# Attention loop of a graph kernel: the front scan turned inside the window sums, next queries ahead of the averaged values, destination indices loaded a group sooner

## The chip, the core and the metric

The kernel runs on one core of a Trainium2 chip. The metric is the device time of one execution in microseconds (us); lower is better. Engines are named as in the profile: PE is TensorE (PEld its weight loads), DVE VectorE, ACT ScalarE, POOL GpSimd, SP SyncE, which issues most DMAs.

## What is computed

3125 nodes of 128 features and 53125 edges sorted by destination (25000 edges both ways and the self loops). Layer 0 is graph attention with 8 heads of 16; layer 1 a degree-normalised sum with a hyperbolic map. Cut to layer 0, which is where the change lies:

```python
h = jnp.maximum(_layernorm(x), 0.0)
Q, K, V = (h @ Wq + bq), (h @ Wk + bk), (h @ Wv + bv)          # (3125, 8, 16) each
scores = jnp.sum(Q[dst] * K[src], axis=-1) * scale + (edge_attr @ We + be)
exp_s = jnp.exp(scores - segment_max(scores, dst)[dst])
probs = exp_s / (segment_sum(exp_s, dst) + 1e-10)[dst]
x = x + segment_sum(probs[:, :, None] * V[src], dst) @ Wo + bo
```

Layer 1 follows with the same edges: `x + expmap0(segment_sum(h1[src] * dinv[src] * dinv[dst], dst))`.

## The kernel before

The edges are cut into 32 groups (`GROUPS`) of 13 tiles (`T`) of 128 edges. One lap of the attention loop handles one group g, and the engines work on it side by side, joined by semaphores alone; each engine's order is written out by hand in its own `step`.

**POOL** (`gather`) fetches K and V of each edge's source: 13 indirect DMAs of 128 rows of 1 KB per group, in chunks of 4, 4, 4 and 1 tiles (`CH`), into `kv[:, b]` with b = g % 2. Below, gather 0 to gather 12 are those of one group. Ahead of gather 7 it waits until gathers 4 to 6 have landed (line 667). Ahead of gathers 0 and 8 it waits for `s_wv`, that is until `weigh(g - 2)` has read that half of the buffer.

**PE** turns the window's 128 query rows into one row per edge (`query`, `ps_q <- ST, qwin`), in four chunks, adds the edge bias (`bias`), and sums the weighted values of group g-1 by destination (`window_sums`, 13 tiles of two passes each, then the two small carry products that set `s_rc`). It counts source degrees (`ps_f <- oh_lo, oh_hi`) and turns small tiles for the scans.

**DVE** in `step(g)`: `scores` multiplies and reduces chunk by chunk (`prod`, `sc`), adds the bias and scans the running maximum of each head over the 13 tiles (`f1`); `scan_partitions` scans over the 128 partitions, `backward`, `scan_partitions_back` and `shifted` do the same from the other end, so that `z` is the score less its segment's maximum. `combine` carries the sums R of group g-1 and averages them (`agn`); it also held the one-hot matrices of a coming group: `shift_matrix`, `edge_one_hots` and `row_one_hots` (`ST <- dloc_b, imj`). ACT takes the exponent, and `weigh` multiplies V by it in two pieces (`wv <- kv, wv`). `new_rows(g - 1)` adds the residual once PE has made the product with Wo (`s_o`).

**SP** loads for the coming groups, in a loop whose every step also stores the rows of group g-2 and so waits for `new_rows`: edge features, `dloc_b` (destination indices spread over 128 partitions), query rows, then the store, then the residual rows.

Of the kernel before, what the change touches and what calls it, by code (L numbers as in the profile page):

```python
# [27 lines left out]
P = 128  # L28
# [23 lines left out]
TB = CH[2][0]  # L52

# [73 lines left out]
def build(nc, x, src_t, dst_t, dst_before, dst_after, dst_first, dst_run, src_run, attr, wqkv, bqkv, we, be, wo, bo, w1t, b1,  # L127
# [12 lines left out]
    with ExitStack() as ctx:  # L140
# [331 lines left out]
        def _(sp):  # L472
# [49 lines left out]
            def load_edges(g, b):  # L522

                if not (known(g) and g < 2):
                    wait_apart(sp, s_bias, g - 1, (s_base, 1))
                sp.dma_start(attr_s[:, b, 0:3, :],
                             attr[bass.ds(g, 1), 0:3 * P, :].rearrange("o (k p) e -> p (o k) e", p=P)).then_inc(s_attr[b], 16)
                sp.dma_start(attr_s[0:EF, b, 3, :],
                             attr[bass.ds(g, 1), 3 * P:T * EF, :].rearrange("o p e -> p (o e)")).then_inc(s_attr[b], 16)
                load_dloc(g, b)  # L530
                w = base_of(g)
                if not (known(g) and g < 2):
                    wait_apart(sp, s_qt, NCH * (g - 1), (s_base, 1))
                sp.dma_start(qwin[:, b, :], q_tab[bass.ds(w, P), :]).then_inc(s_qwin[b], 16)
# [17 lines left out]
            with sp.If_eq(in_order, 1):  # L552
                load_edges(0, 0)
                load_edges(1, 1)
                load_nodes(0, 0)
# [4 lines left out]
                with sp.Fori(1, GROUPS // 2) as n:  # L560
                    for b in range(2):
                        load_edges(2 * n + b, b)
                        store_nodes(2 * n + b - 2, b)
                        load_nodes(2 * n + b, b)
# [160 lines left out]
        def _(dve):  # L725
# [200 lines left out]
            def scores(g, b, st, more):  # L926
# [88 lines left out]
            def combine(g, b, st, edges, more, next_st):  # L1015

# [4 lines left out]
                if more:  # L1021
                    shift_matrix(g + 2, b, s_rc, s_S)
# [4 lines left out]
                if more:  # L1027
                    edge_one_hots(g + 2, b, s_S, TA)
                    row_one_hots(g + 2, b)
                st.sync()  # L1030
                V.tensor_tensor(R[:, b, :], R[:, b, :], ps_r[:, 0:C + 1], ALU.add).then_inc(s_R, 1)
                if edges:
                    scan_partitions(g + 1, 1 - b, next_st)
                dve.wait_ge(s_R, g + 1)
                r3 = R[:, b, 0:C].rearrange("p (h e) -> p h e", h=H)
                st.mark(V.tensor_scalar(rden[:].unsqueeze(2), r3[:, :, DH:DH + 1], 1e-10, None, ALU.add))
                if edges:
                    first_row(g + 1, next_st)
                st.sync()
# [19 lines left out]
            def step(g, b, edges=True, nodes=True, more=True, far=True):  # L1059
# [3 lines left out]
                if edges:  # L1063
                    scores(g, b, A, more)
                if nodes:
                    combine(g - 1, 1 - b, B, edges, edges and more, A)
                    B.check(NB)
                else:
                    scan_partitions(g, b, A)
                    first_row(g, A)  # L1070
                    shift_matrix(g + 1, 1 - b, s_rc, s_S)
                    edge_one_hots(g + 1, 1 - b, s_S, TA)
                    row_one_hots(g + 1, 1 - b)
# [6 lines left out]
                if nodes:  # L1080
                    new_rows(g - 1, 1 - b)
# [275 lines left out]
        def _(act):  # L1357
# [42 lines left out]
            def step(g, b, nodes=True, more=True):  # L1400
                if more:
                    one_hots(g + 1, 1 - b, (0, 1))
                if nodes:
# [3 lines left out]
                carry_factor(g)  # L1407
                weights(g)
# [90 lines left out]
        def _(pe):  # L1499
# [58 lines left out]
            def window_sums(g, b, bias_read=True):  # L1558
# [11 lines left out]
                if bias_read:  # L1570
# [5 lines left out]
            def step(g, b, edges=True, nodes=True, more=True):  # L1576
                if edges:
                    query(g, b, (2, 3))
                if nodes:
                    window_sums(g - 1, 1 - b, edges)  # L1580
                if edges:

# [7 lines left out]
                    pe.wait_ge(s_v1, g + 1)  # L1590
                    M.transpose(p_v1, f1[:, :, T - 1], ident[:]).then_inc(s_v1T, 1)
                if edges:
                    wait_apart(pe, s_cf, g + 1, (s_part, 1))
                    M.transpose(p_c1, c1[:, b, 0:P], ident[0:H, 0:H]).then_inc(s_cfT, 1)
                if nodes:
                    pe.wait_ge(s_agn, g)
                    M.transpose(ps_f[:, 0:D], agn[:], ident[:]).then_inc(s_agTp, 1)
                if edges:
# [3 lines left out]
                    M.transpose(p_c2, c2[:, 1:P + 1], ident[0:H, 0:H]).then_inc(s_cbT, 1)  # L1602
                if nodes:
# [5 lines left out]
                if edges and more:  # L1609
                    query(g + 1, 1 - b, (0,))  # L1610
                    bias(g + 1, 1 - b, (0, 1))
                    query(g + 1, 1 - b, (1,))
# [171 lines left out]
```

## Time and profile before

| | us |
|---|---|
| median of three runs (lowest, highest) | 1085.56 (1083.99, 1094.68) |
| the profiled execution | 1088.42 |
| its span in the trace | 1086.2 |
| first gather of the attention loop starts | 48.90 |
| last gather of the attention loop starts | 709.46 |
| busy in the span: PE, PEld, DVE, ACT, POOL | 883.0, 734.1, 734.9, 394.2, 656.0 |

The attention loop takes from 48.90 to about 735 of the span; what follows is layer 1, which the change doesn't touch. In the rows of a timeline the columns are start, duration, engine, line, operation, output and inputs, and in brackets how long the engine had been idle and for what. The busy shares are averages over both layers, so the loop is read from its own stretches.

### The profile page before, as it was taken

What the parts mean: (1) busy time and instruction counts of PE and PEld (TensorE: products, weight loads), DVE (VectorE), ACT (ScalarE), POOL (GpSimd) and SP (SyncE); (2) the same over time, 40 slices, a digit from 0 to 9 for tenths busy, and PEclk for the clock granted to TensorE, in tenths of its full rate; (3) what the DMA queues carried; (4) which work ended last, traced back from release to release, by engine and by line L of the source; (5) the groups of instructions that cost most, each with busy time, mean ns of one, the idle gap of its engine ahead of it and who ended that gap; (6) DMA issues with size and microseconds to landing.
All of it is one profiled execution on the core that took longest, in us unless ns stands there. A gap on an engine that the chain in (4) does not pass through costs nothing.

```text
span 1086.2 us, 20358 instructions
## 1 busy us (share of the span) xinstructions
PE 883.0 (81%) x4860; PEld 734.1 (68%) x4860; DVE 734.9 (68%) x2772; ACT 394.2 (36%) x1091; POOL 656.0 (60%) x629
## 2 busy tenths in 40 slices
PE   4548878888897988887987898873479999999996
PEld 2237867876886886886876787772267575757574
DVE  8746576576666666666657657748857676768675
ACT  1532233233223224224223323302725565556551
POOL 0167767766776676776776776610267666667663
PEclk9866676676666666667667667676789999999999
DMA  5553443443443443443444353401212222222221
GB/s 151 168 169 91 137 118 108 144 118 110 134 126 108 130 132 108 126 135 113 119 137 117 107 146 114 115 26 65 79 49 60 64 59 61 60 60 60 63 61 47
DMA packets 87845, 111.18 MB, mean 102 GB/s; under 512 B 20787, under 2 KB 65791, under 8 KB 87807
## 3 DMA queue, kind: packets, MB, share of 16 engines
q0 software_dynamic: 26624, 68.20, 21.8%
q1 hardware_dynamic: 61191, 42.64, 13.9%
q8 instruction: 12, 0.20, 0.1%
q14 instruction: 18, 0.15, 0.0%
HBM read 99.83 MB, written 10.95 MB: 102 GB/s over the span
## 4 chain that ended last, share of the span: by engine, by line
POOL 25%; PE 23%; issue 19%; DVE 16%; DMA 14%; ACT 1%; DVEq 1%; POOLq 0%; ACTq 0%; SPq 0%
POOL kv L668 18%; DMA kv<-kv_tab,idx 10%; POOL kv L703 7%; PE ps_r L1697 5%; PE ps_f L1705 3%; PE ps_q L1554 2%; PE ps_r L1566 2%; DMA kv<-hs_tab,idx 2%; PE ps_s L1680 2%; PE ps_q L1680 2%; DVE ST L880 2%; DVE wv L1012 1%; DVE sc L941 1%; PE ps_f L1608 1%; PE ps_f L1607 1%
## 5 line engine op out<-in xcount | busy, mean ns | idle before, releaser
L668 POOL DMA_INDIRECT kv<-kv_tab,idx x416 | 458.3, 1102 | 251.2 <-issue 167.8
L703 POOL DMA_INDIRECT kv<-hs_tab,idx x208 | 197.3, 949 | 166.2 <-DMA hs_tab<-qkv 69.5
L1378 ACT ACTIVATE S<-iota,nloc 128x128 f32<-128x128 f32 x384 | 122.1, 389 | 383.0 <-PE ps_r L1566 381.9
L1554 PE MATMUL ps_q<-qwin,ST 128*128 128x128 f32 x832 | 205.5, 430 | 2.0 <-DVE ST L880 2.0
L935 DVE TENSOR_TENSOR prod<-kv,ps_q 128x512 f32<-128x512 f32 (+1 forms) x128 | 74.6, 583 | 172.8 <-DMA kv<-kv_tab,idx 103.9
L1554 PEld LDWEIGHTS ps_q<-qwin,ST 128*128 128x128 f32 x832 | 186.1, 329 | 3.0 <-issue 2.1
L1566 PE MATMUL ps_r<-wv,S 128*128 128x137 f32 x832 | 140.8, 342 | 1.8 <-DVE wv L1012 1.8
L1566 PEld LDWEIGHTS ps_r<-wv,S 128*128 128x128 f32 x832 | 140.7, 254 | 2.1 <-DVE wv L1012 2.1
L1697 PE MATMUL ps_r<-qkv,xt 128*128 128x128 f32 x800 | 101.7, 292 | 21.2 <-ACT xt L1468 21.2
L1697 PEld LDWEIGHTS ps_r<-qkv,xt 128*128 128x128 f32 x800 | 98.7, 206 | 27.4 <-ACT xt L1468 25.6
L1538 PEld LDWEIGHTS ps_c<-we,attr_s 128*128 128x128 f32 (+1 forms) x256 | 62.9, 321 | 19.9 <-DMA attr_s<-in_attr 12.1
L1538 PE MATMUL ps_c<-we,attr_s 128*128 128x32 f32 (+1 forms) x256 | 65.8, 378 | 11.8 <-DMA attr_s<-in_attr 11.8
L941 DVE TENSOR_REDUCE sc<-prod 128x32 f32<-128x512 f32 (+1 forms) x128 | 71.5, 580 | 0.0
L1457 ACT ACTIVATE S<-iota,nloc 128x128 f32<-128x128 f32 x208 | 67.1, 392 | 0.0
L1012 DVE TENSOR_TENSOR wv<-kv,wv 128x1024 f32<-128x1024 f32 x64 | 62.1, 1007 | 0.2 <-ACT wv L1397 0.2
L1381 ACT ACTIVATE S<-S 128x512 f32<-128x512 f32 x96 | 60.5, 630 | 3.0
L1587 PE MATMUL ps_f<-oh_lo,oh_hi 128*50 128x64 bf16 x416 | 56.8, 303 | 0.0
L1705 PE MATMUL ps_f<-kv,S 128*128 128x128 f32 x416 | 51.0, 281 | 3.8 <-DMA kv<-hs_tab,idx 3.7
L1283 DVE TENSOR_SCALAR ST<-bwd_reset 128x800 bf16<-128x800 f16 x112 | 50.3, 449 | 4.5 <-PE ps_c L1680 4.5
L1284 DVE TENSOR_SCALAR wv<-iota_b,bwd_reset 128x128 bf16<-128x128 bf16 x208 | 52.5, 252 | 0.0
L1705 PEld LDWEIGHTS ps_f<-kv,S 128*128 128x128 f32 x416 | 49.3, 197 | 4.5 <-issue 3.6
L1587 PEld LDWEIGHTS ps_f<-oh_lo,oh_hi 128*50 128x50 bf16 x416 | 49.0, 172 | 0.8
(245 smaller groups left out, 1282.7 us busy)
## 6 DMA issues: line engine op xcount, KB each, us to landing
dloc_b<-dloc_tab SPq DMA_DIRECT2D x32, 416.0 KB, 5.1
kv<-kv_tab,idx POOLq DMA_INDIRECT x416, 4.0
attr_s<-in_attr SPq DMA_DIRECT2D x32, 192.0 KB, 2.9
kv<-hs_tab,idx POOLq DMA_INDIRECT x208
kv_tab<-qkv SPq DMA_DIRECT2D x5, 640.0 KB, 4.0
x_tab<-x SPq DMA_DIRECT2D x32, 64.5 KB
qwin<-q_tab SPq DMA_DIRECT2D x32, 64.0 KB, 4.1
xwin<-in_x SPq DMA_DIRECT2D x32, 64.0 KB, 2.0
```

The source lines that it names most:

```text
L668: pool.indirect_dma_start(out=kv[:, b, t, :], out_offset=None, in_=kv_tab, in_offset=bass.IndirectOffsetOnAxis(ap=idx[:, b, t:t + 1], axis ...
L703: pool.indirect_dma_start(out=kv[:, j, t, 0:D], out_offset=None, in_=hs_tab, in_offset=bass.IndirectOffsetOnAxis(ap=idx[:, j, t:t + 1], ax ...
L935: V.tensor_tensor(prod[:, c % 2, 0:w, :], kv[:, b, t0:t1, 0:D], ps_q[c % 2][:, 0:w * D].rearrange("p (t d) -> p t d", d=D), ALU.mult).then ...
L941: st.mark(V.tensor_reduce(sc[:, :, t0:t1].rearrange("p h t -> p t h"), prod[:, c % 2, 0:t1 - t0, :].rearrange("p t (h d) -> p t h d", d=DH ...
L1012: V.tensor_tensor(w4[:, t0:t1, :, 0:DH], kv[:, b, t0:t1, D:2 * D].rearrange("p t (h d) -> p t h d", d=DH), w4[:, t0:t1, :, DH:DH + 1].to_b ...
L1378: A.activation(S[:, b, t, :], iota[:], ACT.Abs, bias=nloc[:, g, t:t + 1] if known(g) else nloc[:, bass.ds(g, 1), t:t + 1].rearrange("p g t ...
L1538: mm = M.matmul(p_bias[:, 4 * H * k:4 * H * k + w], attr_s[0:r, b, k, :], we4[0:r, 0:w], start=False, stop=k == 3)
L1554: mm = M.matmul(ps_q[c % 2][:, (t - t0) * D:(t - t0 + 1) * D], ST[:, b, t, :], qwin[:, b, :], start=True, stop=True)
L1566: mm = M.matmul(ps_r[:, 0:C + 1], S[:, b, t, :], wv[:, t, :], start=(t == 0), stop=(t == T - 1))
L1587: mm = M.matmul(ps_f[0:HI, 3 * D:3 * D + LO], oh_hi[:, b, :, t], oh_lo[:, b, :, t], start=(t == 0), stop=(t == T - 1))
L1697: M.matmul(ps_r[:, 0:D], counts[:, i, :], hs_t[:, i, :], start=(i == 0), stop=False)
L1705: M.matmul(sum_banks[1][:, 0:D], S[:, j, t, :], kv[:, j, t, 0:D], start=(t == 0), stop=False)
```

## The change

In the PE's `window_sums(g - 1)` the transpose of group g's front scan (`f1`) is put ahead of the last two of the 13 tiles; before it stood behind the degree counts. The counts now stand behind the transpose of the partition scan. `query(g + 1, chunk 0)` is put ahead of the transpose of `agn`, and the product with Wo behind `query(g + 1, chunk 1)`. DVE takes the partition scan before the carry, the averaging behind `z`, `weigh` right behind the averaging, and the one-hots of the edges, `first_row`, `shift_matrix` and `new_rows` behind `weigh`. `row_one_hots` moves to the start of a step, behind the first product, and makes them for group g+1 there (before: for group g+1 in `combine` of the same step). ACT takes `carry_factor` and `weights` ahead of `agg_copy` and the last third of the one-hots. SP issues the load of `dloc_b` for group g+1 where it issued that for group g. No instruction is added or taken out of a lap.

```diff
+TV = T - 2
@@ SP
-                load_dloc(g, b)
...
+                def turn(g, b, more=True):
+                    if more:
+                        load_dloc(g + 1, 1 - b)
+                    load_edges(g, b)
+                    store_nodes(g - 2, b)
+                    load_nodes(g, b)
@@ DVE scores
                 product(0)
+                if more:
+                    row_one_hots(g + 1, 1 - b)
@@ DVE step
                 if edges:
                     scores(g, b, A, more)
+                if edges:
+                    scan_partitions(g, b, A)
                 if nodes:
-                    combine(g - 1, 1 - b, B, edges, edges and more, A)
...
+                    carry(g - 1, 1 - b, B)
                 if edges:
                     backward(g, b, A)
+                if nodes:
+                    add_sums(g - 1, 1 - b, B)
...
                     shifted(g, b, A)
                 if nodes:
+                    average(g - 1, 1 - b, B)
+                    B.check(NB)
+                if edges:
+                    weigh(g, b)
+                    first_row(g, A)
+                    if more:
+                        shift_matrix(g + 1, 1 - b, s_rc, s_S)
+                        edge_one_hots(g + 1, 1 - b, s_S, TA)
+                if nodes:
                     new_rows(g - 1, 1 - b)
                 if edges:
                     add_counts(g)
                     factor(g)
-                    weigh(g, b)
@@ ACT step
+                carry_factor(g)
+                weights(g)
                 if nodes:
                     agg_copy(g - 1)
                 if more:
                     one_hots(g + 1, 1 - b, (2,))
-                carry_factor(g)
-                weights(g)
@@ PE window_sums
                 for t in range(T):
                     if t == TB:
                         pe.wait_ge(s_wv, 2 * g + 2)
+                    if edges and t == TV:
+                        turned_front(g + 1)
```

DVE, one step of the loop, from the scan to the next product, before (`fb` and `R` are the carry, `rden` and `agn` the average, `x` the new rows):

```order
L957 SCALAR_TENSOR_TENSOR f<-fwd_reset,sc 128x104
L905 TENSOR_TENSOR oh_lo<-lo_f,rep_hi 128x832
...
L880 TENSOR_SCALAR ST<-dloc_b,imj 128x1664
L1031 TENSOR_TENSOR R<-R,ps_r 128x137
L967 COPY c<-c 8x1
...
L999 TENSOR_TENSOR z<-sc,tmp 128x104
L1050 TENSOR_TENSOR x<-ps_f,xwin 128x128
L1051 COPY x<-R 128x1
L912 TENSOR_TENSOR od_s<-od_s,ps_f 50x64
L1004 SCALAR_TENSOR_TENSOR facd<-ident,fac 8x8
L1012 TENSOR_TENSOR wv<-kv,wv 128x8x8x16
```

and the same stretch now, up to the next step's products:

```order
L1012 TENSOR_TENSOR z<-sc,tmp 128x104
L1047 TENSOR_SCALAR rden<-R 128x8
L1048 RECIPROCAL rden<-rden 128x8
L1049 TENSOR_TENSOR agn<-R,rden 128x128
L1025 TENSOR_TENSOR wv<-kv,wv 128x8x8x16
L1025 TENSOR_TENSOR wv<-kv,wv 128x5x8x16
L996 TENSOR_SCALAR isf<-iota,ofirst 8x128
L879 TENSOR_SCALAR shift<-imj,delta 128x128
L883 TENSOR_TENSOR S<-dloc,iota 128x128
L1058 TENSOR_TENSOR x<-ps_f,xwin 128x128
```

`ST` (now line 891) has left the middle of the step for the place between the next step's first two products; `wv` no longer stands behind `x`.

PE, from the end of one step into the next, before:

```order
L1607 MATMUL ps_f<-bo_s,ones_row 128x128
L1608 MATMUL ps_f<-wo_s,agT 128x128
L1554 MATMUL ps_q<-qwin,ST 128x128 x4
```

and now:

```order
L1568 MATMUL ps_q<-qwin,ST 128x128 x4
L1623 MATMUL ps_f<-ident,agn 128x128
L1548 MATMUL ps_c<-be_r,ones_row 128x104
L1549 REGISTER_ALU
L1552 MATMUL ps_c<-we,attr_s 128x32 x2
L1568 MATMUL ps_q<-qwin,ST 128x128 x4
L1630 REGISTER_ALU
L1631 MATMUL ps_f<-bo_s,ones_row 128x128
L1632 MATMUL ps_f<-wo_s,agT 128x128
```

The product with Wo, on which `new_rows` waits, now stands behind two query chunks and half of the bias.

## Rows read from the trace of the kernel before

**Rows 1.** Page, part 4: shares of the chain that ended last, by engine.
```profile
POOL 25%; PE 23%; issue 19%; DVE 16%; DMA 14%; ACT 1%; DVEq 1%; POOLq 0%; ACTq 0%; SPq 0%
```

**Rows 2.** Windows: exactly 24 laps; busy us and (instructions) of each engine, clock, DMA.
```profile
173.12:670.15 497.03, 426.23 (x2114) 380.92 (x2113) 328.76 (x984) 150.12 (x432) 345.31 (x312) 0.66 0.42 123
```

**Rows 3.** Waits in 150 to 700 us: waiter, releaser, us in total, times, longest.
```profile
DVE prod L935 <- DMA kv<-kv_tab,idx: 88.1, 27, 3.8
POOL kv L668 <- DMA kv<-kv_tab,idx: 66.1, 26, 2.9
DVE prod L935 <- PE ps_q L1554: 54.8, 27, 2.2
```

**Rows 4.** Timeline, POOL and DVE, one lap from gather 11 on (origin 418.99).
```profile
418.99 0.95 POOL L668 DMA_INDIRECT kv<-kv_tab,idx  x1 [0.30 <-issue]
...
423.83 0.69 DVE L935 TENSOR_TENSOR prod<-kv,ps_q 128x512 f32<-128x512 f32 x1 [3.35 <-DMA kv<-kv_tab,idx]
...
428.06 1.53 POOL L668 DMA_INDIRECT kv<-kv_tab,idx  x1 [0.30 <-issue]
...
428.40 1.08 DVE L880 TENSOR_SCALAR ST<-dloc_b,imj 128x1664 f32<-128x1664 bf16 x1
...
429.90 0.94 POOL L668 DMA_INDIRECT kv<-kv_tab,idx  x1 [0.30 <-issue]
...
433.40 0.94 POOL L668 DMA_INDIRECT kv<-kv_tab,idx  x1 [2.56 <-DMA kv<-kv_tab,idx]
...
434.69 0.29 DVE L1050 TENSOR_TENSOR x<-ps_f,xwin 128x128 f32<-128x128 f32 x1 [0.52 <-PE ps_f L1608]
...
435.23 1.94 DVE L1012 TENSOR_TENSOR wv<-kv,wv 128x1024 f32<-128x1024 f32 x2
...
435.90 2.09 POOL L668 DMA_INDIRECT kv<-kv_tab,idx  x1 [0.30 <-issue]
```

**Rows 5.** Timeline, POOL and then DVE, gathers 8 and 9 of an earlier lap.
```profile
227.74 0.95 POOL L668 DMA_INDIRECT kv<-kv_tab,idx  x1 [0.30 <-issue]
229.76 1.37 POOL L668 DMA_INDIRECT kv<-kv_tab,idx  x1 [1.08 <-issue]
...
228.35 1.94 DVE L1012 TENSOR_TENSOR wv<-kv,wv 128x1024 f32<-128x1024 f32 x2
```

**Rows 6.** Timeline, SP's DMA issues around gather 11 (a store, `dloc_b`, the query rows).
```profile
414.85 0.35 SPq L549 DMA_DIRECT2D x_tab<-x  x1
...
418.17 0.34 SPq L519 DMA_DIRECT2D dloc_b<-dloc_tab  x1
...
419.47 0.34 SPq L534 DMA_DIRECT2D qwin<-q_tab  x1
```

**Rows 7.** Timeline, PE: window sums, counts, product with Wo, query 0, bias, query 1.
```profile
422.16 4.49 PE L1566 MATMUL ps_r<-wv,S 128*128 128x137 f32 x26
...
427.38 1.78 PE L1587 MATMUL ps_f<-oh_lo,oh_hi 128*50 128x64 bf16 x13
...
433.06 0.78 PE L1607 MATMUL ps_f<-bo_s,ones_row 1*128 1x128 f32 x2
...
434.15 1.83 PEld L1554 LDWEIGHTS ps_q<-qwin,ST 128*128 128x128 f32 x8
...
436.20 0.50 PEld L1534 LDWEIGHTS ps_c<-be_r,ones_row 1*128 1x128 f32 x2 [0.22 <-issue]
...
437.69 1.83 PEld L1554 LDWEIGHTS ps_q<-qwin,ST 128*128 128x128 f32 x8
```

**Rows 8.** Timeline, the end of the loop: last gather, last scan, its transpose, last `weigh`.
```profile
709.46 0.95 POOL L668 DMA_INDIRECT kv<-kv_tab,idx  x1 [0.30 <-issue]
...
714.28 0.37 DVE L957 TENSOR_TENSOR_SCAN f<-fwd_reset,sc 128x104 f32<-128x104 f32 x1
...
718.61 0.28 PE L1591 MATMUL ps_b<-ident,f 128*8 128x128 f32 x1
...
724.13 1.94 DVE L1012 TENSOR_TENSOR wv<-kv,wv 128x1024 f32<-128x1024 f32 x2
```

More of the change, by code:

```diff
@@ L552, in _ @@
             with sp.If_eq(in_order, 1):
+                load_dloc(0, 0)
+                load_dloc(1, 1)
                 load_edges(0, 0)
                 load_edges(1, 1)
+                load_dloc(2, 0)
                 load_nodes(0, 0)
@@ L559, in _ @@
                 sp.dma_start(x2_tab[N:NPAD, :], zero_rows[:]).then_inc(s_pad, 16)
[L560 to L564, printed above, removed]
+                def turn(g, b, more=True):
[4 more added lines that the diff above has]
+                    load_nodes(g, b)
+                with sp.Fori(1, GROUPS // 2 - 1) as n:
+                    turn(2 * n, 0)
+                    turn(2 * n + 1, 1)
+                turn(GROUPS - 2, 0)
+                turn(GROUPS - 1, 1, more=False)
                 store_nodes(GROUPS - 2, 0)
@@ L1013, in weigh, with carry @@
                                     w4[:, t0:t1, :, DH:DH + 1].to_broadcast([P, t1 - t0, H, DH]), ALU.mult).then_inc(s_wv, 1)
-            def combine(g, b, st, edges, more, next_st):
+            def carry(g, b, st):
                 dve.wait_ge(s_rc, g + 1)
@@ L1556, in query, with turned_front, window_sums @@
                     mm.then_inc(s_qt, 1)
-            def window_sums(g, b, bias_read=True):
+            def turned_front(g):
+                pe.wait_ge(s_v1, g + 1)
+                M.transpose(p_v1, f1[:, :, T - 1], ident[:]).then_inc(s_v1T, 1)
+            def window_sums(g, b, edges=True):
                 pe.wait_ge(s_wv, 2 * g + 1)
@@ L1569, in window_sums @@
                     pe.wait_ge(s_R, g)
-                if bias_read:
+                if edges:
                     pe.wait_ge(s_sc, g + 2)
@@ L1580, in step @@
                     window_sums(g - 1, 1 - b, edges)
+                elif edges:
+                    turned_front(g)
                 if edges:
+                    wait_apart(pe, s_cf, g + 1, (s_part, 1))
+                    M.transpose(p_c1, c1[:, b, 0:P], ident[0:H, 0:H]).then_inc(s_cfT, 1)
                     pe.wait_ge(s_oh, 2 * g + 2)
@@ L1589, in step @@
                     mm.then_inc(s_hist, 1)
[L1590 to L1598, printed above, removed]
                     pe.wait_ge(s_v2, g + 1)
@@ L1602, in step @@
                     M.transpose(p_c2, c2[:, 1:P + 1], ident[0:H, 0:H]).then_inc(s_cbT, 1)
+                if edges and more:
+                    query(g + 1, 1 - b, (0,))
+                if nodes:
+                    pe.wait_ge(s_agn, g)
+                    M.transpose(ps_f[:, 0:D], agn[:], ident[:]).then_inc(s_agTp, 1)
+                if edges and more:
+                    bias(g + 1, 1 - b, (0, 1))
+                    query(g + 1, 1 - b, (1,))
                 if nodes:
@@ L1609, in step @@
                 if edges and more:
-                    query(g + 1, 1 - b, (0,))
-                    bias(g + 1, 1 - b, (0, 1))
-                    query(g + 1, 1 - b, (1,))
                     bias(g + 1, 1 - b, (2, 3))
```

22 lines of the change are left out of this document (4 added, 18 removed).

## The prediction, made before the changed kernel was run

> **What bounds the kernel now.** I read the chain of waits first. It gives POOL 25%, PE 23%, issue 19%, DVE 16% [rows 1], and in the loop it runs through DVE's `weigh` back to POOL, which looks like a ring through all engines that a better order could shorten. The other views speak against that. The windows give 24 laps in 497.03 us, 20.71 us a lap, with DVE at 66% and PE, whose busy time is modelled, at 86% [rows 2]. In the waits DVE stands still for landing gathers 88.1 us and for PE's queries 54.8 us, over 5 us a lap, while POOL waits only for its own DMAs, 66.1 us in 26 laps [rows 3]. The timeline shows why. A gather takes 0.95 us and the next starts 0.30 us later, 1.25 in all; gather 7 starts 3.50 us after gather 6, since it waits until that one has landed (429.90 to 433.40) [rows 4]. So a lap of POOL costs 13 x 1.25 = 16.25, plus 3.50 - 1.25 = 2.25, together 18.5 us, whatever the others do. The missing 2.2 us are stretched gathers: in the lap shown 1.53 instead of 0.95 beside `ST`, and 2.09 beside `weigh` [rows 4].
>
> What stretches them is DVE. `weigh` runs from 435.23 to 437.17; the gather that started at 435.90 ends at 437.99, 0.82 behind it [rows 4]. `ST` runs from 428.40 to 429.48; the gather of 428.06 ends at 429.59, 0.11 behind it [rows 4]. A gather already 0.61 us old when `weigh` starts (227.74 against 228.35) is not touched, and the next one is then held: it starts at 229.76 and ends at 231.13, 0.84 behind `weigh` [rows 5]. So POOL sets the lap, and DVE matters only by where these two operations fall upon gathers. I read no wait of POOL on a semaphore of DVE: the buffer that gather 0 of g+2 needs is free when `weigh(g)` has done its first piece (at 16.2 + 1.2 in a lap whose gather 11 is the origin), and that gather starts at 2.5 + 20.6 = 23.1, almost 6 us later.
>
> **Where the moved parts come to lie.** Times from here on are us behind the start of gather 11, and F is when DVE takes the product of chunk 2, for which gather 11 must have landed. Before, F = 423.83 - 418.99 = 4.84 and `weigh` starts at 16.24, which is F + 11.4 [rows 4].
>
> *The scan to `weigh`.* The front scan ends at F + 3.4 as before. PE has reached the eleventh tile by then (see the ring below), so the transpose follows at once (0.28, duration as in [rows 8]); then the last two tiles, 2/13 of 4.49 = 0.7 [rows 7], and the two carry products, about 0.8 by their rows: `s_rc` at F + 5.2. DVE does its partition scan inside that time, the carry by F + 5.7, the correction and the second scan by F + 6.7. The degree counts, 1.8 us [rows 7], now stand on PE from F + 5.3 to 7.1 and hold the second transpose back by 0.4. From that transpose to the end of `z` it took 2.3 us before; that gives F + 9.3, and three averaging operations give F + 10.0 for `weigh`, 1.4 sooner. ACT's exponent is covered by the averaging; ACT's first two thirds of the one-hots, 3.9 us from F + 4.5, end before z is there.
>
> *The queries.* Query 0, bias and query 1 started at 434.15, 436.20 and 437.69 [rows 7], so they take 2.05, 1.49 and about 1.75. They now run from F + 8.2, with the transpose of `agn` (0.35) between: F + 13.9. The Wo product takes 1.5 from its start (433.06) to the read by `x` (434.69) [rows 4, 7], so `new_rows`, which was done before `weigh`, waits until F + 15.4. DVE then is idle for almost 3 us; behind it are queued the counts, the factor and the next step's products.
>
> *The ring.* Product 0 comes at F + 16.1, `ST` from F + 16.8 to F + 17.9, product 1 to F + 18.6, the reduction to F + 19.2, and there the next chunk 2 can be taken. A ring of 19.2 us is below 20.7, so its slack hides the late `new_rows`; of the 5 us of waits in [rows 3] about 1.5 are left. If this cover were gone, each us would count 32 times.
>
> *The DMAs.* SP's burst (store, residual rows, then loads) started at -4.14 and ended with the query rows at 0.48, `dloc_b` at -0.82, just ahead of gather 11's landing [rows 4, 6]. It now follows `new_rows` and starts at F + 16.1 - 20.7 = F - 4.6, some 3 us later. Gather 6, with no burst beside it, lands about 2.7 us after its start, gather 11 needs 4.84 [rows 4]; so F should fall into 3.0 to 4.8. I take 3.6, nearer to the clean one. `dloc_b` itself, issued a lap sooner, has a whole lap to land; nothing waits for it.
>
> *What POOL pays.* For `weigh` at F + 10.0 = 13.6: gather 7 would start at 13.5 to 13.8. If it starts inside `weigh` or less than about 0.3 before it, it ends 0.83 behind it: with F = 3.0 the stall covers part (1.15 lost), with F = 3.7 nothing (2.0 lost). If `weigh` comes later than that, gather 7 is spared and gather 8 pays 1.0 to 1.8. Before, the mean of the gathers beside `weigh` was 1.56 over 25 laps by my count of their starts. I take 1.5. For `ST`, 1.08 long, ending a gather 0.11 behind it: a gather that is s old at its start loses s + 0.24, so 0.24 to 1.1, or nothing if it fell into the stall; it now starts near F + 16.8 = 20.4, close to gather 11, far from the stall. I take 0.6, the 0.59 of the lap shown [rows 4]. Shift and edge one-hots, now right behind `weigh`, and the source one-hots: 0.25, between 0 and 0.5. Sum 2.35 against 2.2 before: a lap of 20.85, +0.14, and over 32 laps +4.5 us.
>
> A rule speaks to this. The Trainium skill (SBUF — State Buffer, section on who interferes with whom) says that a two-input tensor operation takes only the read side shared with GpSimd, that 2-port modes take both, and that the loser is blocked until the other's end, about 0.115 us for the descriptors to finish. For `ST` the trace agrees (0.11); for `weigh` the gather ends 0.82 behind, so it seems to be held at its start. By the page's 0.115 each `weigh` would cost 0.7 less, before and after alike, and the sum would not change.
>
> *The end of the loop.* In the last lap no gathers hold DVE. The last scan starts at 714.28, but its transpose stands behind the sums and the counts and comes at 718.61, 4.0 us after the scan's end; `weigh` follows at 724.13 [rows 8]. With the transpose inside the sums it comes about 0.5 after the scan; the carry, still 1.3 behind, and the rest as above put `weigh` at 721.6. That is 2.5 us, for once on the path, between 1.5 and 3.5.
>
> **The sum** is +4.5 - 2.5 = +2 us. Against the profiled execution (1088.42, span 1086.2) that is 1090.4; against the median of the runs, 1085.56, it is 1087.6, and I predict 1088: no change.
>
> **Rivals.**
> *Faster: the blocks fall well.* If the burst moves out of gather 11's way, F = 3.0, `weigh` costs 1.15, and `ST` finds a gather young (0.24), small ones 0.1: 1.5 instead of 2.2, a lap of 20.0, 32 x -0.71 - 2.5 = -25, 1060 us. For it: F has 1.8 us of room. Against: F must fall by nearly all of it and `ST` be lucky too. Chance 0.22. The ring (19.2) forbids anything below about 1035.
> *Slower: `ST` in the open.* This is the rule of the same page turned on the change: an operation that takes the shared ports should lie where POOL is not working, and the change does the opposite. Before, `ST` at 9.41 lay one gather ahead of the stall; now each `ST` may cost 1.1, with `weigh` upon the start of gather 7 (1.9) and the two one-hots behind it (0.2): 3.2, a lap of 21.7, +32 - 2.5, 1115 us; with half of the laps so, 1101. It decides once the blocks pass 2.65 a lap. Chance 0.18.
> *The change does nothing to the laps*: all of it stays in DVE's slack and only the end gains, 1083. Chance 0.10.
> The forecast keeps 0.50.
>
> **Numbers.** About 1% (11 us) is what a measurement of this kernel can tell from no change. One lap's uncertainty of 0.4 us is 13 us, so the forecast gives 0.07 to faster and 0.05 to slower. Faster 0.07 + 0.20 = 0.27; slower 0.05 + 0.17 = 0.22; same 0.51. The range 1064 to 1108 takes in most of both rivals. The forecast's own range is 1076 to 1100.
>
> **What would show it.** Right: POOL's only wait is still that ahead of gather 7, 3.5 us after gather 6; `weigh` starts 1.4 us sooner behind product 2; `x` waits about 3 us for the Wo product while DVE's wait for landing gathers shrinks; the lap stays at 20.5 to 21.1; `ST` falls beside gathers 10 to 12 and stretches them. Wrong: a wait of gathers 0 or 8 on `weigh`; a ring above 20.7, seen as DVE taking chunk 2 without waiting for its landing; a stall ahead of gather 7 that differs from 3.5 us, because the later burst meets gathers 4 to 6.

## The result: faster, by what `weigh` costs POOL

The changed kernel takes 1062.28 us (median of 4 runs, 1059.48 to 1064.59), the kernel before 1087.67 on the same chip: ratio 0.9753, with a 95% interval of 0.971 to 0.9795. Two further comparisons (`a1_changed` and `a2_changed` below, each beside the kernel before) gave 0.9788 (0.9733 to 0.9844) and 0.9766 (0.9738 to 0.9794). The forecast, 1088 and no change, was wrong; 1062 lies below its range too. It came out close to the rival "the blocks fall well" (1060, chance 0.22), but not for that rival's reason.

The profiled execution has a span of 1061.0 us. Its chain of waits, by engine, against [rows 1]:

```profile
POOL 43%; issue 22%; DMA 14%; PE 11%; DVE 8%; POOLq 1%; ACT 0%; DVEq 0%; SPq 0%; ACTq 0%
```

The chain now runs mostly on POOL and its DMAs; PE and DVE, before 23% and 16%, are down to 11% and 8%. The windows over 24 whole laps (us, then busy us and instructions of PE, PEld, DVE, ACT and POOL, clock, DMA share, GB/s), which answer to [rows 2]:

```profile
171.41:647.38 475.97, 418.74 (x2120) 372.88 (x2119) 337.27 (x986) 150.30 (x432) 325.78 (x312) 0.66 0.46 128
```

A lap takes 475.97 / 24 = 19.83 us instead of 20.71. PE and DVE do the same work (a mean of 17.45 and 14.05 us a lap, before 17.76 and 13.70) at the same granted clock, 0.66. POOL's busy time for the same 312 gathers fell from 345.3 to 325.8 us, 0.81 a lap: nearly all of the 0.88 of the lap. So the gathers themselves became shorter. The waits from 150 to 680 us, against [rows 3]:

```profile
POOL kv L679 <- issue: 99.6, 321, 1.1
DVE x L1058 <- PE ps_f L1632: 85.6, 26, 3.5
POOL kv L679 <- DMA kv<-kv_tab,idx: 68.2, 27, 2.7
...
DVE prod L946 <- DMA kv<-kv_tab,idx: 19.8, 14, 2.7
```

POOL still waits for its own DMAs alone (68.2 us in 27 laps, before 66.1 in 26). DVE's waits have moved from landing gathers (88.1 to 19.8 us) to the Wo product, 3.3 us a lap.

Where a gather became shorter shows in two laps of the timeline, POOL's rows and then DVE's (start, duration, line, names, idle time before it):

```profile
403.09 1.08 POOL L679 DMA_INDIRECT kv<-kv_tab,idx  x1 [0.30 <-issue]
...
409.54 1.50 POOL L679 DMA_INDIRECT kv<-kv_tab,idx  x1 [0.30 <-issue]
...
440.73 1.57 POOL L679 DMA_INDIRECT kv<-kv_tab,idx  x1 [2.51 <-DMA kv<-kv_tab,idx]
...
401.92 0.29 DVE L1049 TENSOR_TENSOR agn<-R,rden 128x128 f32<-128x128 f32 x1
402.13 1.95 DVE L1025 TENSOR_TENSOR wv<-kv,wv 128x1024 f32<-128x1024 f32 x2
...
408.01 0.29 DVE L1058 TENSOR_TENSOR x<-ps_f,xwin 128x128 f32<-128x128 f32 x1 [3.35 <-PE ps_f L1632]
...
409.14 1.07 DVE L891 TENSOR_SCALAR ST<-dloc_b,imj 128x1664 f32<-128x1664 bf16 x1
...
440.26 1.95 DVE L1025 TENSOR_TENSOR wv<-kv,wv 128x1024 f32<-128x1024 f32 x2
```

`weigh` is two operations, one for 8 tiles and one for 5, and the row joins them. The tile's view keeps them apart (shortest, median and longest in ns, first and last start); before, and now:

```profile
L1012 DVE TENSOR_TENSOR wv<-kv,wv x2: 806/1006/1207, 435.2 to 436.4; 128x1024 f32<-128x1024 f32 x1, 128x640 f32<-128x640 f32 x1
```

```profile
L1025 DVE TENSOR_TENSOR wv<-kv,wv x2: 817/1018/1218, 440.3 to 441.4; 128x1024 f32<-128x1024 f32 x1, 128x640 f32<-128x640 f32 x1
```

Now the first piece ends at 440.26 + 1.22 = 441.48 and the gather beside it at 442.30, 0.82 behind the FIRST piece and 0.09 behind the second; the same in the other lap (403.35, 404.17). Before, the gather ended 0.82 behind the SECOND piece, 1.56 behind the first [rows 4]. By the records this holds throughout: before, in 30 of 31 laps with a gather beside `weigh`, it ended 0.83 behind the second piece; now, in 27 of 31, 0.82 behind the first, and in the other 4 it had started only when the second piece had started too, and ended 0.82 behind that. I say that a gather is **held** through both pieces, or is **let in** between them.

What each DVE operation costs POOL, in us a lap (what the gathers beside it last beyond the 0.945 us of an undisturbed one, laps 6 to 30, from the records):

| kernel | `weigh` | `ST` | others | lap |
|---|---|---|---|---|
| before | 1.43 | 0.51 | 0.15 | 20.69 |
| changed | 0.38 | 0.57 | 0.29 | 19.79 |
| changed, `a1_changed` and `a2_changed` | 0.43, 0.52 | 0.59, 0.54 | 0.26, 0.26 | 19.84, 19.87 |

With the prediction's 18.5 us for an undisturbed lap of POOL these rows add up to the laps within 0.1.

### The profile page after: what moved, and what is told of

It is laid out like the page before. It is cut to its first block, busy times and chain, and to the rows that moved or that the text cites. A ratio compares the mean times of both kernels' runs of the same rounds, so it can differ in the third digit from the quotient of the medians.

```text
span 1061.0 us, 20346 instructions
## 1 busy us (share of the span) xinstructions
PE 873.9 (82%) x4860; PEld 724.1 (68%) x4860; DVE 745.2 (70%) x2772; ACT 394.6 (37%) x1091; POOL 631.2 (59%) x629
## 4 chain that ended last, share of the span: by engine, by line
POOL 43%; issue 22%; DMA 14%; PE 11%; DVE 8%; POOLq 1%; ACT 0%; DVEq 0%; SPq 0%; ACTq 0%
POOL kv L679 29%; POOL kv L714 14%; DMA kv<-kv_tab,idx 9%; DMA kv<-hs_tab,idx 4%; PE ps_q L1568 2%; PE ps_r L1587 2%; PE ps_f L1612 1%; DVE st L759 1%; DMA kv_tab<-qkv 1%; PE ps_f L1726 1%; DVE qkv L787 1%; DVE qkv L1281 1%; PE ps_r L1718 1%; PE ps_q L1530 1%; PE ps_f L1631 0%
## 5 line engine op out<-in xcount | busy, mean ns | idle before, releaser
L679 POOL DMA_INDIRECT kv<-kv_tab,idx x416 | 433.6, 1042 | 250.7 <-issue 166.8
L1568 PE MATMUL ps_q<-qwin,ST 128*128 128x128 f32 x832 | 198.6, 418 | 26.7 <-DVE prod L946 23.6
L1568 PEld LDWEIGHTS ps_q<-qwin,ST 128*128 128x128 f32 x832 | 174.3, 311 | 32.1 <-DVE prod L946 24.9
L1587 PE MATMUL ps_r<-wv,S 128*128 128x137 f32 x832 | 145.7, 343 | 0.0
L1587 PEld LDWEIGHTS ps_r<-wv,S 128*128 128x128 f32 x832 | 143.1, 254 | 0.3
L946 DVE TENSOR_TENSOR prod<-kv,ps_q 128x512 f32<-128x512 f32 (+1 forms) x128 | 74.3, 581 | 43.0 <-DMA kv<-kv_tab,idx 29.6
L1058 DVE TENSOR_TENSOR x<-ps_f,xwin 128x128 f32<-128x128 f32 x32 | 9.4, 292 | 101.5 <-PE ps_f L1632 101.5
```

What stands on the lines that cost most here:

```text
L679: pool.indirect_dma_start(out=kv[:, b, t, :], out_offset=None, in_=kv_tab, in_offset=bass.IndirectOffsetOnAxis(ap=idx[:, b, t:t + 1], axis ...
L946: V.tensor_tensor(prod[:, c % 2, 0:w, :], kv[:, b, t0:t1, 0:D], ps_q[c % 2][:, 0:w * D].rearrange("p (t d) -> p t d", d=D), ALU.mult).then ...
L1568: mm = M.matmul(ps_q[c % 2][:, (t - t0) * D:(t - t0 + 1) * D], ST[:, b, t, :], qwin[:, b, :], start=True, stop=True)
```

## The experiments

Each group of kernels ran on one chip with the kernel before beside it. In the first two groups (e1 to e3; e4b, e5, e6, e7) the kernel before took 1184 and 1210 us instead of 1087; why is not known, and the argument uses from them only ratios and which operation a gather's end follows.

### Is it the place of `weigh`, or what is beside it?

**e1**, the kernel before with `weigh` directly behind `z`:

```
                     shifted(g, b, A)
+                    weigh(g, b)
...
-                    weigh(g, b)
```

> The kernel before, with weigh alone moved: right behind z, ahead of new_rows, the counts and the factor. Theory 'sooner': the lap shrinks by what weigh gains on the landing of gather 11 (about 0.65 us, since it still waits for ACT's exponent), 31 laps, so -20 us. Theory 'port between the pieces': in the kernel before a gather caught by weigh ends 0.82 behind its second piece, in the changed kernel 0.82 behind its first; weigh here starts after an idle gap, as in the one lap of before where the gather did end 0.82 behind the first piece, so I expect that here in all laps, 0.74 a lap, -20 to -28 us. The trace tells them apart: end of the caught gather against the ends of the two pieces.

Ratio 1.0163 (1.009 to 1.0235). The three gathers that `weigh` held up ended 0.82 behind the first piece: let in, in the old order. Yet it was slower: `weigh` fell beside gathers 12 and 0, and gather 0 waited for the semaphore of `weigh`'s first piece, 74.7 us in 27 laps over the kernel. The prediction had given that gate almost 6 us of room.

**e2**, the kernel before with `add_counts` between the two pieces of `weigh`:

> The kernel before, with add_counts (one SBUF input, one PSUM input) moved in between the two pieces of weigh; weigh starts 0.13 us sooner, its second piece ends as before or 0.1 later. 'Port between the pieces': the held gather gets through after the first piece, 0.74 less a lap, -20 to -25 us (about 1064). 'Sooner': 0.1 a lap at most, 1085. 'POOL waits for the semaphore of weigh's first piece': 0.1 a lap too, 1085.

Ratio 1.0032 (0.9989 to 1.0074), and the gathers were held to 0.83 behind the second piece all the same. So a foreign operation between the pieces does not let them in.

**e3**, the kernel before with `factor` and `add_counts` exchanged:

> The kernel before, with factor and add_counts swapped, so that weigh follows the counts instead of the 8x8 factor operation, at the same time. If the operation right ahead of weigh decides whether the port is let go between the pieces: 0.74 less a lap, about 1064. 'Sooner' and 'semaphore': no change, 1086.

Ratio 0.9983 (0.9941 to 1.0025), held as before in 25 laps.

**e4b**, the changed kernel with two short operations directly ahead of `weigh` (PE takes the factor together with the row mask, so both had to move):

```
                 if edges:
+                    first_row(g, A)
+                    factor(g)
                     weigh(g, b)
-                    first_row(g, A)
...
-                    factor(g)
```

> The changed kernel with the row mask (first_row) and factor moved from behind new_rows to directly ahead of weigh; everything else as changed. Before the change a gather caught by weigh ended 0.83 us behind weigh's SECOND piece in 30 of 31 laps, after it 0.82 us behind the FIRST piece in 27 of 31; what stands directly ahead of weigh on DVE differs (before: factor, an 8 x 8 operation; after: the averaging product, 128 x 128). Theory A (what runs directly ahead of weigh decides whether a caught gather gets through between the pieces): factor is ahead again, the caught gathers end 0.83 behind the second piece, the first piece lasts 1.207 instead of 1.219, the lap grows by 0.5 to 0.75 us and the time by 15 to 24 us, to 1077 to 1086. Rival B (it is the place of weigh in the lap, beside gathers 7 to 10 in the open part, that decides): the gathers go on ending 0.82 behind the first piece, and the time stays within 6 us of the changed kernel, 1062.

The hold came back, longer than before. Timeline of one lap:

```profile
300.46 2.50 POOL L679 DMA_INDIRECT kv<-kv_tab,idx  x1 [0.30 <-issue]
...
299.79 1.94 DVE L1025 TENSOR_TENSOR wv<-kv,wv 128x1024 f32<-128x1024 f32 x2
301.66 0.27 DVE L879 TENSOR_SCALAR shift<-imj,delta 128x128 f32<-128x128 f32 x1
301.86 0.27 DVE L883 TENSOR_TENSOR S<-dloc,iota 128x128 f32<-128x128 f32 x1
```

The gather ended at 302.96: 1.23 behind `weigh`, 0.83 behind `S`, the last of the operations queued without a gap behind it. So in 30 laps. Only in the first lap, where `weigh` stood behind a gap, was the gather let in. Ratio 0.9867 (0.9789 to 0.9946).

**e7**, the kernel before with the averaging product repeated into a spare tile directly ahead of `weigh`:

> The kernel before with one operation added: the averaging product done a second time, into a spare tile, directly ahead of weigh and behind factor (0.2 us of DVE a lap, nobody reads it). Theory A (the operation directly ahead of weigh decides whether a caught gather gets through between weigh's pieces): the caught gathers now end 0.82 behind the first piece, the first piece lasts 1.219 instead of 1.207, and the lap falls by 0.5 to 0.75 us: 1065 to 1073, faster than before although an operation was added. Rival B (only the place in the lap or the order of the other steps matters): they still end 0.83 behind the second piece, and the time is that of before within 6 us, 1082 to 1094.

Theory A, as put there, fell: the seven gathers caught behind the first lap were held to the end of the second piece. The kernel was faster (0.9773, 0.9688 to 0.9858); in the profiled execution `weigh` caught a gather in only 8 laps and cost 0.23 us a lap. I draw nothing from that ratio.

### What decides

**e8**, the kernel before with `factor` behind `weigh`:

> The kernel before with factor (an 8 x 8 scalar_tensor_tensor) moved from directly ahead of weigh to directly behind it. So far a caught gather was held through every operation queued behind a factor (before: to the end of weigh's second piece; with factor ahead of weigh in the changed kernel: even to the end of the edge one-hots, 1.22 behind weigh, in 30 of 32 laps), also where another operation stood between factor and weigh (the spare product, the counts); without factor ahead (the changed kernel) it got through at the end of the first piece. Theory A (the factor's operation makes DVE keep the gathers out until a chain of back-to-back operations ends): here weigh has no factor ahead, caught gathers end 0.82 behind the FIRST piece, the lap falls by up to 0.74 us; where weigh lies beside gathers at all, that is 10 to 24 us less than before, ratio 0.98 to 0.99. Rival (something else in the order of the changed kernel lets them through): they still end 0.83 behind the second piece, ratio 0.995 to 1.005.

Held as before in 28 laps, ratio 0.9977 (0.9954 to 0.9999): theory A fell again. It isn't the factor. Ahead of `weigh` now stood `x`, its copy and the counts, without a gap. Behind `weigh` the factor and product 0 followed without a gap either, and yet the gather ended 0.82 behind `weigh` and not behind them.

**e9**, the changed kernel with one short operation more:

```
+                    V.scalar_tensor_tensor(out=spare[:], in0=ident[0:H, 0:H], scalar=imj[0:H, 0:1],
+                                           in1=ident[0:H, 0:H], op0=ALU.mult, op1=ALU.subtract)
                     weigh(g, b)
```

> The changed kernel with one 8 x 8 scalar_tensor_tensor on constants, written to a spare tile and read by nobody, added directly ahead of weigh (0.14 us of DVE a lap). Theory A (that operation makes DVE keep the gathers out): caught gathers end 0.8 us behind the end of the edge one-hots (1.22 behind weigh's second piece) instead of behind the first piece, so each costs up to 1.1 us more: the lap grows by 0.7 to 1.1 us, the time by 20 to 35 us against the changed kernel. Rival (only the place of weigh matters): the ends stay at 0.82 behind the first piece and the time within 6 us of the changed kernel.

1081.0 us where the changed kernel of the same group took 1062.9: an operation of 0.21 us on 8 x 8 numbers that nobody reads costs 18 us. The timeline:

```profile
184.91 2.51 POOL L680 DMA_INDIRECT kv<-kv_tab,idx  x1 [2.46 <-DMA kv<-kv_tab,idx]
...
184.23 0.29 DVE L1050 TENSOR_TENSOR agn<-R,rden 128x128 f32<-128x128 f32 x1
184.44 0.21 DVE L1091 SCALAR_TENSOR_TENSOR spare<-ident,imj 8x8 f32<-8x8 f32 x1
184.57 1.94 DVE L1026 TENSOR_TENSOR wv<-kv,wv 128x1024 f32<-128x1024 f32 x2
```

The gather ends at 187.42, 0.91 behind `weigh` (I had said 1.22), so in 30 laps, and `weigh` costs POOL 1.39 us a lap again; `ST` 0.55, as in the changed kernel.

**e12**, the kernel before with one wait, by which `weigh` starts behind a gap:

```
                     factor(g)
+                    dve.wait_ge(s_facd, g + 1)
                     weigh(g, b)
```

> The kernel before with one wait added: weigh's first piece waits for the semaphore that factor, the operation directly ahead of it, raises at its end. No work is added or moved. In the kernels in which a caught gather was held to the end of weigh (before, e4b, e7, e8, e9) two or more short operations ran back-to-back directly ahead of weigh's first piece; where weigh came behind an idle gap (first laps, e1) or behind one operation that had a gap ahead (the changed kernel) the gather got through at the end of the piece. Theory A (the run without a gap decides): the wait opens a gap of some 0.03 us, the caught gathers end 0.82 behind the FIRST piece, and the lap falls by 0.5 to 0.75 us; the kernel before is 15 to 24 us faster by one added wait: 1062 to 1073 where before is 1086. Rival (the neighbours or the order of the changed kernel are needed): caught gathers end 0.83 behind the second piece, ratio 0.997 to 1.004.

Right as to the mechanism. Two laps, early and late:

```profile
186.00 1.62 POOL L668 DMA_INDIRECT kv<-kv_tab,idx  x1 [0.31 <-issue]
...
185.34 0.21 DVE L1004 SCALAR_TENSOR_TENSOR facd<-ident,fac 8x8 f32<-8x8 f32 x1
185.58 1.96 DVE L1012 TENSOR_TENSOR wv<-kv,wv 128x1024 f32<-128x1024 f32 x2
...
330.31 0.95 POOL L668 DMA_INDIRECT kv<-kv_tab,idx  x1 [2.12 <-DVE wv L1012]
...
328.32 1.96 DVE L1012 TENSOR_TENSOR wv<-kv,wv 128x1024 f32<-128x1024 f32 x2
```

The factor ends at 185.55, `weigh` starts 0.03 later, its first piece (1.226) ends at 186.81 and the gather at 187.62: let in, as in all 9 laps in which one was caught (one of them the first, which lets it in before as well). Wrong as to the size: 0.9941 (0.9921 to 0.9961), 6 us and not 20. POOL, now faster, ran up to the ring of engines. From lap 10 on `weigh` lies beside gathers 12 and 0, gather 0 waits for its first piece (35.7 us in 21 laps), and the lap stays at 20.44 us, where 18.5 and the stretched gathers alone (0.09 for `weigh`, about 0.55 for the rest) would give 19.1.

So there are two causes, and they need each other. From `weigh` to `weigh`, 31 laps:

| | held | let in |
|---|---|---|
| old order | 20.74 (before) | 20.44 (e12) |
| new order | 20.54 (e9) | 19.85 (changed; 19.72 and 19.77 in `a1_changed` and `a2_changed`) |

Each cell is one profiled execution, and that of e9 (1085.4) was 4.4 us above its median, 0.14 a lap. In times: letting the gather in gave 6 us in the old order (e12), the new order without it 5 us (e9, 1081.0 against 1086.3), and the two together 23 (1062.9).

### The size of the hold

**e14** and **e10**, the changed kernel with `weigh` in one operation, and in four (4, 4, 3 and 2 tiles):

> The changed kernel with weigh as one operation over all 13 tiles (about 1.95 us) instead of two pieces; its semaphore is raised by two at its end, so the window sums start 0.75 us later than behind the first piece. Theory A (a caught gather is held to the end of the operation that catches it): the mean price of weigh rises from 0.5 to 1.0 to 1.5 us a lap, +16 to +30 us against the changed kernel (1062), back to 1078 to 1092. Rival (the price hangs on where weigh lies, not on its pieces): within 6 us of the changed kernel.

> The changed kernel with weigh in four operations instead of two (4, 4, 3 and 2 tiles; the semaphore is still raised twice, behind the second and the fourth). Theory A (in the changed kernel a caught gather gets through at the end of the piece that holds it): pieces of about 0.6 us let it go sooner, the mean price of weigh falls from 0.5 to 0.3 us a lap, and the time by 3 to 8 us against the changed kernel; the four operations last 0.1 to 0.2 us longer together. Rival (the hold is that of the whole of weigh): no gain, 0 to 5 us slower by the longer weigh.

e14: 1075.6 us, ratio 0.9875 (0.9842 to 0.9908), `weigh` 1.09 us a lap. e10: 1057.2, ratio 0.9723 (0.9668 to 0.9777), `weigh` 0.19. The timeline of e14, then of e10:

```profile
83.56 2.63 POOL L679 DMA_INDIRECT kv<-kv_tab,idx  x1 [2.60 <-DMA kv<-kv_tab,idx]
...
83.48 1.89 DVE L1024 TENSOR_TENSOR wv<-kv,wv 128x1664 f32<-128x1664 f32 x1 [0.53 <-ACT wv L1410]
```

```profile
202.08 1.24 POOL L679 DMA_INDIRECT kv<-kv_tab,idx  x1 [2.47 <-DMA kv<-kv_tab,idx]
...
201.81 2.10 DVE L1025 TENSOR_TENSOR wv<-kv,wv 128x512 f32<-128x512 f32 x4
```

With one piece the gather ends at 86.19, 0.82 behind its end. With four it ends at 203.32, 0.82 behind the first of them (0.69 long), while `weigh` runs on to 203.91. So pieces with no gap between them don't keep a gather out by themselves. The price goes with the length of the piece: 1.09, 0.38 to 0.52, 0.19 for one, two and four. `a1_changed` is the changed kernel beside e8 to e10 (1062.9, 0.9788); the four runs of e10 all lie below its four, though the intervals of the ratios overlap:

> The changed kernel as it is, to have it on the same chip as the three above. Ratio to before 0.96 to 0.985; caught gathers end 0.82 behind weigh's first piece.

**e11** and **e11b**, e10 with `ST` in three operations too, twice; the second time beside `a2_changed`, the changed kernel as it is:

> The changed kernel with weigh in four operations (as e10, 1057) and ST in three (5, 4 and 4 tiles; its semaphore raised behind the last). Gathers beside ST cost 0.7 us a lap in e10 (gathers 11 to 1). Theory A (a caught gather is let go at the end of the piece): that price falls to 0.3, and the time by 5 to 12 us against e10, to 1045 to 1052. Rival (the three pieces of 0.4 us are a run without a gap, through which the gather is held to the end, as with weigh in the kernel before): no gain, 1055 to 1062.

> The version with weigh in four operations and ST in three again, beside the changed kernel on the same chip. It had 1054.0 where the changed kernel had 1062 to 1063 on other chips. Theory A (a let-go gather pays by the length of the operation that catches it): 5 to 12 us faster than the changed kernel. Rival (the difference was that of the chips): within 3 us of it.

> The changed kernel as it is, beside e11b and e6n on the same chip: 1060 to 1065 us, ratio to before 0.973 to 0.98.

1054.0 (0.9701, 0.9677 to 0.9726) and 1054.5 (0.9697, 0.9679 to 0.9714), the changed kernel 1061.1 beside it (0.9766): 6.6 us faster, with intervals that don't touch. Most of that is e10's 5.7; `ST` costs 0.56 us a lap in e11b, not clearly less than in the changed kernel, and e11 against e10 is not settled (they ran in different groups, and their intervals overlap).

### The other parts of the change

**e5** and **e5n**, the kernel before with `ST` behind product 0 and the indices a group sooner, alone; the first in the group where before took 1210 us, the second where it took 1087:

> The kernel before with one part of the change alone: the source one-hot comparison ST behind product 0 instead of ahead of the partition scan, and the destination indices loaded a group sooner. Weigh and its neighbours as before. Theory A (most of the gain is what POOL pays for weigh, 0.74 us a lap): this alone gives at most 5 us; ratio 0.995 to 1.01, caught gathers end 0.83 behind weigh's second piece. Rival (ST's place is the gain: before it stretched gather 9 or 10 by 0.6, now it lies elsewhere): a gain of 8 to 20 us, ratio 0.98 to 0.992. The rival of the prediction that ST in the open costs 1.1 a lap: a loss of 10 us or more.

> The kernel of e5_st_alone again, for a chip on which the kernel before takes about 1086 us: the kernel before with ST behind product 0 and the destination indices a group sooner, all else as before. Theory A (the gain lies in what weigh costs): within 6 us of before, ratio 0.995 to 1.006. Rival (ST's place is a good part of the gain): ratio 0.985 to 0.993.

1.0038 (0.9987 to 1.0088), and 1.010 (1.0083 to 1.0117), which is 11 us slower. The first lies within what theory A allowed; the second lies outside both ranges of its expectation and is the loss that e5's third possibility named. The timeline of e5n:

```profile
124.51 3.23 POOL L677 DMA_INDIRECT kv<-kv_tab,idx  x1 [0.30 <-issue]
...
124.08 1.94 DVE L1023 TENSOR_TENSOR wv<-kv,wv 128x1024 f32<-128x1024 f32 x2
125.95 0.67 DVE L944 TENSOR_TENSOR prod<-kv,ps_q 128x512 f32<-128x512 f32 x1
126.55 1.07 DVE L889 TENSOR_SCALAR ST<-dloc_b,imj 128x1664 f32<-128x1664 bf16 x1
```

The gather ends at 127.74, 1.72 behind `weigh` and 0.12 behind `ST`; so in 28 laps. This need not be one long hold. In two laps the gather ended 0.82 and 0.83 behind `weigh`, in one of them with product 0 alone queued without a gap behind it; and a gather under way when `ST` begins ends 0.12 behind it in the kernel before too (11 laps). So the likelier reading, not tested by itself, is that the gather is let go at the end of `weigh` and caught again by `ST`, which begins 0.53 us later. The two cost 2.20 us a lap together, before 1.94. That explains the direction but not all of the 11 us: the profiled execution was the fastest of the five (1091.3), and its lap is only 0.10 longer than before. In the changed kernel the 3.3 us of waiting for Wo stand between `weigh` and `ST`. F, the start of DVE's product of chunk 2 behind gather 11, fell to 2.96 us in the median of e5n (before 4.76), and it gained nothing: DVE's wait was slack.

**e6** and **e6n**, the changed kernel with the Wo product ahead of query 1, the first in the group of e5, the second where before took 1089:

> The changed kernel with PE's Wo product ahead of query 1 instead of behind it, so that new_rows gets its input 1.5 to 1.8 us sooner. In the changed kernel DVE waits 3.3 us a lap for that product (88.5 us). Theory A (POOL sets the lap, DVE's wait is slack): DVE's wait falls by 1 to 2 us a lap, the time stays within 6 us of 1062, up or down with where the operations fall upon gathers. Rival (the ring of the engines sets the lap): each us of wait taken away comes off the lap, 30 us and more: below 1035.

> The kernel of e6_wo_ahead again, for a chip on which the kernel before takes about 1087 us: the changed kernel with PE's Wo product ahead of query 1 instead of behind it. Theory A (POOL sets the lap of the changed kernel; DVE's 3.3 us of waiting for this product are slack): the wait falls by 1 to 2 us a lap and the time stays within 6 us of 1062. Rival B (the ring of the engines sets it): the time falls below 1045. Rival C (what the last runs suggest: query 1, now behind the Wo product, comes later, the next products with it, and ST and weigh slide towards gather 0, which then waits for weigh): the lap grows by 0.3 to 1 us, 1072 to 1094, with waits of gather 0 on weigh in the trace.

e6: 1.0444 (1.0361 to 1.0528), with gather 0 waiting for `weigh`. But in eight laps `x` itself had waited 11 to 13 us for something that no engine of the core released; its other waits are below 2.5 us:

```profile
POOL kv L679 <- DVE wv L1025: 103.8, 13, 11.3
DVE x L1058 <- remote: 95.5, 8, 12.9
```

What came late there isn't shown, and so neither that the order is to blame. e6n has no such wait: 1059.7, the changed kernel of its group 1061.1, the same. Its waits over the whole kernel, against 101.5 us for `x` in the changed kernel:

```profile
DVE prod L946 <- DMA kv<-kv_tab,idx: 74.9, 37, 4.9
DVE x L1058 <- PE ps_f L1631: 47.9, 32, 2.3
```

Half of the wait for Wo was taken away and turned into waits for landing gathers (29.6 us in the changed kernel): slack, as the forecast said. POOL alone sets the lap of the changed kernel.

## The prediction, step by step

- *POOL sets the lap, 18.5 us free-running, and stretched gathers make the rest*: right. Gather 7 starts 3.47 us behind gather 6 in the median (before 3.90, since there `ST` often stretched gather 6 itself), and the lap minus 18.5 is the sum of the prices.
- *`weigh` at F + 10.0*: the median is F + 10.0 (before F + 11.5). F itself was taken as 3.6 within 3.0 to 4.8; its median is 4.4 (before 4.8), and some laps reach 7.0.
- *`x` waits almost 3 us for Wo, hidden*: 3.35 in the lap shown, and e6n showed that it is hidden.
- *`ST` costs 0.6, small ones 0.25*: measured 0.57 and 0.29. The size was right, the rule behind it only in part, which is luck: that `ST` ends a gather 0.11 behind it holds in 12 of 32 laps before and 6 of 31 now, with a gather that was under way when `ST` began or started in its first 0.06 us; in the other 20 and 25 it ends 0.82 behind. The rival "`ST` in the open" was wrong for the change as a whole, though e5n shows that this part alone costs 11 us.
- ***`weigh` costs 1.5 us a lap*: this step failed.** It costs 0.38 (0.43 and 0.52 in the two further comparisons), so the lap came out at 19.8 and not 20.85. I took the mean of the kernel before (read as 1.56, by the records 1.43) as a property of `weigh`; I had listed where in each lap a gather starts, and never asked which operation its end follows. The trace held the hint: `weigh` is two operations, and in the first lap, where it stood behind a gap, the gather of 82.16 ended 0.82 behind the first.
- *`weigh`'s place mattered only for how it falls upon gathers; the gate on gather 0 has 6 us of room*: wrong for the old order, which e12 brought to that gate at 20.44, just 0.3 below its lap. For the new order I had put the ring at 19.2; e11b ran at 19.50 with no wait of POOL on DVE, so it is not above that.
- *The end of the loop gains 2.5 us*: it lost 1.7. From the last gather to `weigh` it is 14.25 us, before 14.67; and from `weigh` to the last copy behind `x` 12.3, before 10.25. The end of the loop now, DVE and then PE, against [rows 8]:

```profile
686.04 0.29 DVE L1058 TENSOR_TENSOR x<-ps_f,xwin 128x128 f32<-128x128 f32 x1 [2.97 <-PE ps_f L1632]
...
692.36 0.37 DVE L970 TENSOR_TENSOR_SCAN f<-fwd_reset,sc 128x104 f32<-128x104 f32 x1
...
698.45 1.95 DVE L1025 TENSOR_TENSOR wv<-kv,wv 128x1024 f32<-128x1024 f32 x2
...
692.94 0.27 PE L1575 MATMUL ps_b<-ident,f 128*8 128x128 f32 x1
...
700.14 0.80 PE L1632 MATMUL ps_f<-wo_s,agT 128*128 128x128 f32 x2
700.73 5.17 PE L1587 MATMUL ps_r<-wv,S 128*128 128x137 f32 x26
```

The transpose does follow the scan at once, as forecast. But the scan comes 8.2 us behind the last gather, not 4.8, since `x` waited 2.97 us for Wo, here on the path; and the last sums stand behind another Wo product on PE. What is slack in the loop is not at its end.

The sum: predicted +4.5 for the laps and -2.5 for the end; measured -25.5 from the first to the last gather, and +1.7; the rest of the kernel, which the change doesn't touch, came out about 1.6 shorter. The time of the rival "the blocks fall well" was right by luck. Its mechanism (F = 3.0 and a lucky `ST`) did not happen: F came to 4.4 and `ST` cost what it cost before. One sum is off and changes nothing: half of the laps at +1.0, less 2.5 for the end, give 1099 and not 1101.

## What to carry to other kernels

Where gathers are issued by POOL beside DVE work, list for each stretched gather which DVE operation its end follows, and not only its duration: that tells whether it is held for one operation or for several. Then two small edits are worth a trial: one wait that opens a gap of 0.03 us ahead of the long operation (6 us in the old order, e12), and the long operation in pieces (5.7 us on top of the change, e10). Before counting such a gain, price the ring that waits behind the first bound; in the old order it left 6 us of the 20 that I had expected of the wait.

## What the runs showed of the hardware

A gather that starts inside a two-input operation of DVE ends 0.82 us behind the end of an operation, but of which one depends on how DVE came to it. One rule tells the held kernels from the others. Behind an idle gap, or behind one operation that had a gap ahead (the changed kernel's `agn`), the gather is let in at the end of the operation that caught it (before in its first lap, changed, e1, e6, e6n, e10, e12, e14). Behind two or more short operations (0.14 to 0.29 us) without a gap it is held beyond that (before, e2, e3, e4b, e5, e5n, e7, e8, e9). The run ahead and what stands behind `weigh`, in the kernel before (the lap of [rows 4]):

```profile
434.90 0.14 DVE L1051 COPY x<-R 128x1 f32<-128x1 f32 x1
434.96 0.20 DVE L912 TENSOR_TENSOR od_s<-od_s,ps_f 50x64 f32<-50x64 f32 x1
435.09 0.21 DVE L1004 SCALAR_TENSOR_TENSOR facd<-ident,fac 8x8 f32<-8x8 f32 x1
435.23 1.94 DVE L1012 TENSOR_TENSOR wv<-kv,wv 128x1024 f32<-128x1024 f32 x2
437.10 0.67 DVE L935 TENSOR_TENSOR prod<-kv,ps_q 128x512 f32<-128x512 f32 x1
```

How far the hold reaches, no rule found here says. It is not to the end of the run: product 0 stands without a gap behind `weigh`, and the gather ends at 437.99, 0.82 behind `weigh` (before, e2, e3, e7, and e8 with the factor between). In e4b it reaches over two operations more, to `S`, and in e9 the gather ends 0.91 behind `weigh`, 0.82 behind the end of no operation. The records differ too, but don't decide: in most let-in laps the second piece starts 0.082 to 0.086 us before the first has ended, in held ones 0.070 to 0.078; 7 let-in laps of the changed kernel have 0.075 to 0.077. That a gap decides is shown by e12, that one short operation decides by e9; what happens inside DVE, and why two are enough, stays open.

The Trainium skill (SBUF — State Buffer, who interferes with whom) says that a DVE instruction with two SBUF inputs contends with a GpSimd instruction that reads SBUF, and of DVE's 2-port modes that who issues first has the shared pair "for the whole instruction". Where gathers are let in, the trace agrees for `weigh` as well; in the held laps it was for both pieces, in e2 with the degree counts between them (`od_s<-od_s,ps_f`, one input in PSUM), which by the page don't contend.

POOL's gather of group g+2 into a buffer that `weigh(g)` reads is a real gate: where it binds, the gather starts 0.75 us behind the end of `weigh`'s first piece (e12: 328.32 + 1.23 + 0.75 = 330.30).
